# Transformer block on image tokens: maxima placed by one transfer, q and k of a tile by one, columns reordered where they are made

## What is computed

```python
h = concat([cls_tok, cls_token, patches @ W_lin.T + b_lin])          # (64, 198, 192)
q, k, v = heads(layernorm(h) @ w_qkv.T)                              # 12 heads of 16
attn = softmax(rope(q * 16 ** -0.5) @ rope(k).T)
h = h + (attn @ v) @ w_proj.T + b_proj
h = h + ffn(layernorm(h))
# ffn: bitlinear (rmsnorm, 8-bit rounding of x, ternary weights) 192 -> 2 x 512, silu(gate) * up, bitlinear 512 -> 192
```

## Time and profile before

| what | value |
|---|---|
| runs | 1248.65, 1253.7, 1248.05 us; median 1248.65 |
| the profiled execution | 1248.7 us (its span) |
| PE (TensorE) busy | 1185.9 us, 95% |
| VectorE, ScalarE, GpSimd busy | 959.7, 871.2, 891.6 us |
| the 16 DMA engines | 39.1% of their time on SP's queue |
| chain that ended last | PE 76%, DMA 7%, VectorE 5%, SP's queue 5% |

### The profile page before, as it was taken

One profiled execution on the slowest core, in us unless ns is written; L12 is line 12 of the kernel. 1 busy time (PEld: TensorE's weight loads), 2 busy tenths in 40 slices (PEclk: granted clock), 3 DMA queues, 4 the chain that ended last, 5 costly groups with the idle time before them and its releaser, 6 DMA issues.

```text
span 1248.7 us, 36954 instructions
## 1 busy us (share of the span) xinstructions
PE 1185.9 (95%) x12229; PEld 847.2 (68%) x12229; DVE 959.7 (77%) x2335; ACT 871.2 (70%) x1736; POOL 891.6 (71%) x1605
## 2 busy tenths in 40 slices
PE   7689999999899999999999999999999999999887
PEld 6466766767676677677667766776767677766566
DVE  3455777788688888788788888887788778888786
ACT  1145667677577777777877777777677677777686
POOL 3755676777577787777887777877677678777354
PEclk9889999999899999999999999999899899999999
DMA  7534432544344443444444444344344434432110
GB/s 195 137 88 115 111 96 71 124 116 103 87 108 125 122 102 96 115 127 100 114 107 123 106 102 107 101 125 107 104 111 99 109 95 119 105 78 66 45 48 30
DMA packets 203948, 129.19 MB, mean 103 GB/s; under 512 B 57449, under 2 KB 203060, under 8 KB 203668
## 3 DMA queue, kind: packets, MB, share of 16 engines
q1 hardware_dynamic: 201188, 123.71, 39.1%
q10 hardware_dynamic: 2576, 3.14, 0.9%
HBM read 66.57 MB, written 10.70 MB: 62 GB/s over the span
## 4 chain that ended last, share of the span: by engine, by line
PE 76%; DMA 7%; DVE 5%; SPq 5%; issue 3%; ACT 3%; POOL 2%; ACTq 0%; POOLq 0%; DVEq 0%
PE turn L537 14%; PE score L595 12%; PE turn L617 10%; PE turn L555 9%; PE turn L646 6%; PE score L575 5%; PE turn L604 4%; DMA qkT<-nmaxT 4%; PE turn L625 3%; DVE nmax L937 3%; PE turn L626 2%; PE turn L563 2%; PE turn L664 2%; PE turn L547 2%; PE turn L519 1%
## 5 line engine op out<-in xcount | busy, mean ns | idle before, releaser
L937 DVE TENSOR_REDUCE nmax<-score 99x8 f32<-99x1584 f32 x192 | 347.3, 1809 | 167.5 <-PE score L575 167.2
L746 ACT ACTIVATE prob<-score 99x1584 f32<-99x1584 f32 x192 | 286.6, 1493 | 105.5 <-PE score L595 104.9
L537 PE MATMUL turn<-wlin,xp 128*128 128x192 f32 x1188 | 231.9, 348 | 7.8 <-DMA xp<-in_x 7.8
L537 PEld LDWEIGHTS turn<-wlin,xp 128*128 128x128 f32 x1188 | 203.1, 200 | 18.0 <-issue 8.9
L595 PE MATMUL score<-qkT 32*99 32x198 f32 x3072 | 181.3, 351 | 20.9 <-DMA qkT<-nmaxT 13.2
L617 PE MATMUL turn<-prob,vaug 99*32 99x198 f32 x3072 | 169.5, 340 | 0.0
L1122 POOL TENSOR_TENSOR yg<-early,gout 128x512 f32<-128x512 f32 x99 | 125.9, 1272 | 56.0 <-ACT yr L810 50.7
L595 PEld LDWEIGHTS score<-qkT 32*99 32x99 f32 x3072 | 117.2, 162 | 64.5 <-issue 38.8
L555 PE MATMUL turn<-wqkv,xT 96*128 96x384 f32 x396 | 151.6, 505 | 0.0
L769 ACT ACTIVATE xiT<-turn 96x256 bf16<-96x256 bf16 x99 | 37.6, 380 | 131.8 <-PE turn L635 131.6
L617 PEld LDWEIGHTS turn<-prob,vaug 99*32 99x32 f32 x3072 | 81.2, 110 | 64.3 <-issue 37.5
(11 more groups left out here) (94 smaller groups left out, 2408.6 us busy)
## 6 DMA issues: line engine op xcount, KB each, us to landing
xp<-in_x SPq DMA_DIRECT2D x63, 588.0 KB, 5.3
qkT<-qkd SPq DMA_DIRECT2D x168, 96.0 KB, 2.3
tab<-joined SPq DMA_DIRECT2D x98, 112.0 KB, 3.0
orec<-rden_kept SPq DMA_DIRECT2D x192, 49.5 KB
out<-h SPq DMA_DIRECT2D x99, 96.0 KB, 3.4
onum<-osb SPq DMA_DIRECT2D x64, 99.0 KB, 2.6
vaug<-vt SPq DMA_DIRECT2D x30, 148.5 KB
onum<-osb SPq DMA_DIRECT2D x64, 49.5 KB, 2.3
```

The source lines that it names most:

```text
L537: last = pe.matmul(turn[:, k, 0:D], xp[:, c, place:place + TILE], wlin[:, c, :], start=(c == 0), stop=(c == KC - 1))
L746: act.activation(prob[:, :, 4 * g:4 * g + 4, :].rearrange("p t r n -> p r t n"), score[0:TT, :, 0:2 * TOKENS].rearrange("p r (t n) -> p r ...
L937: dve.tensor_reduce(nmax[:, b % 2, :, 4 * g:4 * g + 4].rearrange("p t r -> p r t"), score[0:TT, :, 0:2 * TOKENS].rearrange("p r (t n) -> p ...
```

## The change

Place_max issues one transfer of 12 rows instead of three of 4. For that nmax keeps its heads in another order: column 3 r + g instead of 4 g + r for head r of group g, so that the 12 transposed rows run as the destination does, band by band and in each band group by group.

Place_qk issues one transfer of 128 partitions for a piece instead of two of 64. For that POOL's last rope operation writes qkp's columns in another order (q and k alternating), so that partition 2 d + h of chunk c holds number d of group c of q (h = 0) or k (h = 1).

The counts on the semaphores qk_placed and nmax_placed follow: 16 per piece instead of 32, 16 per image instead of 48. Nothing else differs.

```diff
--- before.py
+++ after.py
@@ -118,7 +118,7 @@
 
 def qk_count(i):
 
-    return sum(32 * len(pieces(TILE * n, TILE, QRING)) for n in range(i % 2, i + 1, 2))
+    return sum(16 * len(pieces(TILE * n, TILE, QRING)) for n in range(i % 2, i + 1, 2))
 
 
 def beyond(i):
@@ -398,9 +398,8 @@
                 if over >= 0:
                     sp.wait_ge(st_ready, 3 * over + 3)
                 for place, lo, n in pieces(TILE * i, TILE, QRING):
-                    for half in range(2):
-                        sp.dma_start(qkT[0:128:2, half:2 * GROUPS:2, place:place + n],
-                                     qkd[64 * half:64 * half + 64, i % 2, :, lo:lo + n]).then_inc(qk_placed[i % 2], 16)
+                    sp.dma_start(qkT[0:128:2, :, place:place + n],
+                                 qkd[:, i % 2, :, lo:lo + n]).then_inc(qk_placed[i % 2], 16)
 
             def place_o(b):
 
@@ -433,9 +432,8 @@
             def place_max(b):
                 sp.wait_ge(nmaxT_copied, b + 1)
                 place = TOKENS * b % QRING
-                for g in range(GROUPS):
-                    sp.dma_start(qkT[31:128:32, g, place:place + TOKENS], nmaxT[4 * g:4 * g + 4, b % 2, :])\
-                        .then_inc(nmax_placed[b % 2], 16)
+                sp.dma_start(qkT[31:128:32, 0:GROUPS, place:place + TOKENS], nmaxT[:, b % 2, :])\
+                    .then_inc(nmax_placed[b % 2], 16)
 
             def store(i):
                 sp.wait_ge(out_ready, i + 1)
@@ -586,7 +584,7 @@
 
             def exp_scores(n):
                 b, g = divmod(n, GROUPS)
-                pe.wait_ge(nmax_placed[b % 2], 16 * GROUPS * (b // 2 + 1))
+                pe.wait_ge(nmax_placed[b % 2], 16 * (b // 2 + 1))
                 take_score(exp_done, n + 1)
                 place = TOKENS * b % QRING
                 for t in range(2):
@@ -735,7 +733,7 @@
             def copy_maxT(b):
                 act.wait_ge(nmaxT_ready, b + 1)
                 if b >= 2:
-                    act.wait_ge(nmax_placed[b % 2], 16 * GROUPS * (b // 2))
+                    act.wait_ge(nmax_placed[b % 2], 16 * (b // 2))
                 act.activation(nmaxT[:, b % 2, :], turn[0:HEADS, bank_of["nmaxT", b], 0:TOKENS], ACT.Copy).then_inc(nmaxT_copied, 1)
 
             def exps(n):
@@ -934,7 +932,7 @@
                 dve.wait_ge(maxin_ready, n + 1)
                 if b >= 2:
                     dve.wait_ge(nmaxT_ready, b - 1)
-                dve.tensor_reduce(nmax[:, b % 2, :, 4 * g:4 * g + 4].rearrange("p t r -> p r t"),
+                dve.tensor_reduce(nmax[:, b % 2, :, g:HEADS:GROUPS].rearrange("p t r -> p r t"),
                                   score[0:TT, :, 0:2 * TOKENS].rearrange("p r (t n) -> p r t n", t=2),
                                   AX.X, ALU.max, negate=True).then_inc(max_done, 1)
 
@@ -1097,7 +1095,9 @@
                 pool.wait_ge(rope_parts, 2 * i + 2)
                 if i >= 2:
                     pool.wait_ge(qkT_ready, i - 1)
-                pool.tensor_tensor(qkp[:, i % 2, :], ropec[:, :], ropes[:, :], ALU.add).then_inc(rope_done, 1)
+                pool.tensor_tensor(qkp[:, i % 2, :].rearrange("p (c d h) -> p h c d", c=GROUPS, h=2),
+                                   *(r[:, :].rearrange("p (h c d) -> p h c d", c=GROUPS, h=2) for r in (ropec, ropes)),
+                                   ALU.add).then_inc(rope_done, 1)
 
             def round_qkT(i):
                 pool.wait_ge(qk_placed[i % 2], qk_count(i))
```

## The result

The changed kernel takes 1230.18 us in the median (1228.96 to 1232.13), the kernel before 1251.18 us beside it (1248.05 to 1262.48). The ratio is 0.9846, 95% interval 0.9805 to 0.9887: 1.5% faster, some 20 us. The profiled executions, 1248.7 and 1227.2 us, differ by 21.5.

What follows compares the result with a forecast made beforehand. TensorE was taken to bound the steady stretch, leaving its idle time and the clock to win. 1248.7 less 4.3 us idle and 4.9 clock gave 1239.5, stated as 1240 us; range 1230 to 1249, the forecast's own 1236 to 1243.

Steps and rivals of the forecast that it cites:

- rival (b): Issue of the maxima sets their arrival: each wait loses 1.7 us or all; 1230 us, to 1226; chance 0.13.
- The bound and the place: Steady stretch, 140 to 1120 us: TensorE bound; only 16.7 us idle and 17.1 of clock winnable; start and tail 0.
- The seven waits are set by v's rows in one DMA queue: Transfer of maxima into qkT: four rows stand behind v's; arrival is place_v's start plus 8.4 to 11.4 us.
- own sign for (b): Steps of tiles 62 and 73: maxima landing sooner than 8.4 and 11.1 us after place_v starts would show rival (b).
- Place_max at 0: One maxima transfer for three: SP free 1.06 us sooner per image, but 0 for PE in the seven steps.
- Place_qk at 0.55 a wait: One q and k transfer for two: place_v starts 0.63 us sooner; each wait loses 0.55, ends 0.3 and 0.65.
- rival (d): SP's own pauses fall elsewhere, lengthening waits and adding slow stretches; 1260 us at worst, 1256 typical; chance 0.06.
- The clock at 4.9: Slow-clock windows around tiles 14 and 82 return to the upper level as waits shrink: 4.9 us, bounds 0 to 8.4.
- The price of a fall: Half clock does half the work: a window loses its length times one minus mean clock; 17.1 us in five.
- The costs at nothing: Reordered columns at the producers: POOL's stepped add 0, upper end one microsecond; VectorE 0; TensorE and ScalarE unchanged.
- rival (c): The merged q and k transfer takes as long to issue as two; gain 0 to 1 us, 1248 us; chance 0.07.
- (e): POOL's stepped add costs over 3.7 us instead of 1.0, in each of 99 steps; 1300 us and up; chance 0.02.

Runs made afterwards that it cites:

- one issue put back: Changed kernel with one small extra transfer (16 rows of 16 bytes to device memory) ahead of each place_v; 1237.47 us, ratio 0.9883 to the kernel before.

## Why the prediction was right, and where it was too small

**The number.** The time lies at the very end of the stated range: 1230.18 us in 1230 to 1249. It is 10 us below the forecast of 1240 and outside the forecast's own 1236 to 1243, and the gain was some 20 us where 9.2 had been summed. The ratio taken on 1248.7 would give 1229.5, outside. That the range held it is owed to the near half of rival (b) and to luck; the mechanism below is what was right.

**The bound and the place.** Right. The gain is PE's idle time in the rounds named, some in the rounding's waits, and the clock after them; start and tail gave nothing, they are 1.5 us longer.

**The seven waits are set by v's rows in one DMA queue.** Right, and now shown rather than argued. The arrival in tile 73's step moved only from 11.11 to 10.89 us after place_v, though the last issue of maxima now starts 2.10 us after place_v for 4.20. Cutting v's runs removed every such wait, in both kernels. With v in 292 transfers PE is idle for 2.1 us of 960, and with the 226 of the kernel before for 16.7 of 980.

The trace's records of single DMA packets show the queue itself. In tile 73's step of the kernel before, v's 128 rows of 1536 bytes are moved one after another, 65 ns each, from 863.68 to 872.43 us. Of the maxima's twelve rows nine have been moved by 867.82, and the last three go right behind v's last row, from 872.43 to 872.55. The changed kernel has the same picture: v from 847.79 to 856.54, nine of the maxima's rows by 850.84, the last three from 856.54 to 856.65. By the rule of the Trainium skill (DMA: Bandwidth & Descriptors, section on why a DMA increments its semaphore by 16), 61, 67 or 83 rows go over one queue. The trace agrees: in this step v's 61 and 67 rows go one at a time.

A long first queue is needed for such a wait but isn't enough. In five more steps, of tiles 36, 39, 56, 59 and 70, the maxima follow place_v with 82 to 90 rows on that queue by the same count, and PE doesn't wait for them: it starts their scores only 8.7 to 11.1 us after place_v, when they have landed. The waits depend on the start of place_v, the length of the queue and the moment at which PE asks.

Rival (b), 1230, had the right time by a reason that is wrong in the main: with one issue fewer ahead of v and the maxima still in three, 1232.46 us are reached. The prediction's own sign for (b), an arrival sooner than 8.4 and 11.1 us after place_v, did come in part, by 0.41 and 0.22 us; the next step is where that belongs.

**Place_max at 0.** Wrong. The step reasoned that what stands behind v's rows gains nothing from fewer issues. Alone the merge gave 0.7%: the waits for the maxima fell by 4.2 us in sum. Part of it is the 0.40 us on the arrival, measured above in three steps (seven of them would be 2.8). The rest may be that SP is 1.06 us further on after each image; no run takes the two apart. The 0.40 us do not lie on the crowded queue, where the step was right: in tile 73's step the maxima's last row has been moved 10.2 us after the start of place_v, whether in three transfers or in one. They lie behind it: from the end of that row to the start of the scores 0.96 us pass in the kernel before (873.51 - 872.55) and 0.57 with the maxima alone merged (864.58 - 864.01). Why one transfer's end is told sooner than that of three is not settled: I did not try two transfers, or other sizes.

**Place_qk at 0.55 a wait.** The mechanism is right, the size too small. The seven waits lost 1.42, 1.60, 0.77, 1.59, 0.49, 1.46 and 0.86 us, 8.2 together, where I had 3.8. To the 0.63 us of one issue (0.68 by place_v's start after place_qk in the steps without a pause) comes the 0.40 above, and in tile 73's step a pause of SP that stood ahead of place_v: 2.40 us from place_qk to place_v before, 846.47 - 845.32 = 1.15 now. I had named such pauses as a danger (rival (d)) and not as something that the change could take away. The rounding's waits lost 2.7 us, not 0.5; 1.86 of it is the one at 215.66, which is gone. Together the idle time was put at 4.3 us and fell by 10.6 over the stretch.

**The clock at 4.9.** Too small again: 12.4 us. I let two of five slow windows go; four went, those around the waits of 1.66, 1.86, 2.70 and 1.97 us, and the fifth's loss shrank from 5.2 us (40 x 0.13) to 3.5 (35 x 0.10). Around the two that remain above 1 us, 1.24 and 1.11, the clock now stays at the upper level. So the one error, the size of the cut in each wait, probably came in twice; but that the length of the wait alone decides about the fall is not shown, and one row speaks against it. In the run with one issue put back the wait of tile 25's step is 2.61 us, and no fall follows:

```profile
306.73 0.93 PE L605 MATMUL score<-qkT 32*99 32x198 f32 x16 [2.61 <-DMA qkT<-nmaxT]
...
290.00:325.00 35.00, 32.39 (x359) 23.09 (x357) 28.29 (x66) 24.41 (x51) 25.07 (x45) 1.00 0.38 106
```

The falls also differ from one execution to the next of one and the same kernel. In 23 executions beside the first experiments the kernel before took 1234.67 to 1263.31 us, at a mean granted clock of 0.993 in the fastest and 0.970 in the slowest. So 12.4 us is what one execution of each kernel gives, and part of it may be chance. The price of a fall was about right: the lower level stands for 27.2 us less, 13.6 us by the prediction's rule of one half, and 12.4 were measured; the same 16 matmuls take 0.93 us at the upper level and 1.61 or 1.66 behind two of the waits.

With the measured 10.6 us of idle time and 12.4 for the clock the sum would have been 1248.7 - 23.0 = 1225.7, and start and tail gave 1.5 back: 1227.2, as measured.

**The costs at nothing.** POOL's add takes 1013 ns for 1010: right. The merged transfer of q and k is issued in 622 ns and lands in 2.5 us for 2.3: the rival (c) falls. The merged transfer of the maxima takes 602 ns for 528. Neither (d) nor (e) came.

## What to carry to other kernels

Where a small transfer lands late on a DMA system that is 40% busy, look at what stands ahead of it in its own queue, and how many queues that was spread over: 128 rows on one queue held up the last three rows of the maxima for some 8 us (128 x 65 ns), and with 66 transfers more, none of them long on one queue, the kernel was faster. Fewer issues on SP helped here by moving the start of the long transfer, not by making the short one cheaper. And count a stall on a saturated TensorE with the slow clock behind it: in the two executions profiled here that part, 12.4 us, was worth more than the idle time, 10.6.

## What the runs showed of the hardware

Two transfers of 61 and 67 rows of 1536 bytes were moved row after row, 65 ns each, while the 16 DMA engines were busy 34% of the time on average, and a transfer of 4 rows issued behind them ended behind them. Before, 42 rows more on the queue cost 2.71 us, the same 65 ns a row. A transfer merged from three to one landed 0.40 us sooner though its last row was moved no sooner. In the kernel before, exchanging two transfers in a queue so that the urgent one goes first made the kernel slower by 0.6 to 1.0%; in the stall that was followed, the long one held up what stands behind it instead.
